# Transposes spread singly among the products of a graph network's node and edge steps

## The chip, the cores and the metric

The kernel runs on one core of one Trainium2 chip. The metric is the device time of one execution in microseconds (us); lower is better. One execution was also taken with the hardware profiler, which gives every instruction's start, duration and what ended the idle time before it.

## The reference, cut to what matters

Three layers of a graph network run over 10,000 nodes of 512 features and 5,000 edges, all in 32-bit floats:

```
def _sage_conv(x, src, dst, Wp, bp, Wl, bl, Wr):
    h = jax.nn.relu(x @ Wp.T + bp)
    agg = jax.ops.segment_sum(h[src], dst, num_segments=N)
    cnt = jax.ops.segment_sum(jnp.ones((src.shape[0],), x.dtype), dst, num_segments=N)
    agg = agg / jnp.maximum(cnt, 1.0)[:, None]
    return agg @ Wl.T + bl + x @ Wr.T
...
h = jnp.maximum(_layernorm(x, axis=-1), 0.0)
# three of these in a row; after layers 0 and 1: relu, layernorm, times g, plus be
x = x + (the last layer's result)
```

## The kernel before, in words

**Tiles.** A layer has 79 node tiles of 128 rows and then 40 edge tiles of 125 rows. A node tile is loaded, normalised on ScalarE (`xn`, L697), stored to `node_x` for the edges to gather from, and turned on TensorE: four transposes of 128x128 (`node_turn`, L492; the transposes at L498), one for each chunk of 128 features, into one bank of PSUM. ScalarE rounds the bank to a high part (`xt_high`, L677) and VectorE takes the remainder (`xt_low`, L791 in layer 0, L794 later). The product with Wr (`node_product`, L502) then takes, for each of the four chunks, three matmuls of 512 columns (L512 low times high, L513 high times low, L514 high times high), which add up in one bank. VectorE adds the bias (`node_out`, L835; in layer 2 the residual, L832) and SyncE's queue stores the rows.

**Edge tiles.** An edge tile is gathered by GpSimd (L419) into `rows_in`, turned in the same way (`edge_turn`, L556; transposes at L564), split into high and low (L707, L910 or L913), and used by `project` (L568) in groups of four tiles: each of the four calls for a group makes one quarter of the output features, 12 matmuls at L579 to L581. `edge_product` (L585, 12 matmuls at L598 to L600) and `edge_sum` (L603) follow, then GpSimd adds the rows into the node table (L431), one tile's transfer after the other.

**Order.** Each engine has its own order, written out by hand, and waits on counting semaphores. A node step `i` puts on TensorE: turn tile i+2, product of tile i, and in layer 0 extra work. On ScalarE it puts std of tile i+6, `xt_high` of tile i+2, and the norm of tile i+5. On VectorE it puts `xt_low` of tile i+2 first, then `node_out` of i-1, statistics of i+8, small operations, and in layer 0 the extra work. SyncE's queue stores tile i-1 once `n_out` allows it, and in layer 2 loads the residual of tile i+3 behind the same wait (L338).

**The extra work that matters here.** In layer 0, steps 46 to 65 look up how many edges each edge's node has. TensorE makes two small matmuls a step behind the product (`lookup`, L529, two calls; matmuls at L535), VectorE reads them in its next step (`read_count`, L879, at L881). Call 2j may not start before the reading of call 2j-2 is done, since it writes the same bank:

```
if t >= 2:
    pe.wait_ge(count_read, t - 1)
```

On VectorE step i reads the two calls of step i-1, as the last entries of the step:

```
if l == 0 and STEP_LOOKUP <= i - 1 < STEP_LOOKUP + EDGE_TILES // LOOKUPS:
    for q in range(LOOKUPS):
        read_count((i - 1 - STEP_LOOKUP) * LOOKUPS + q)
```

Of the kernel before, what the change touches and what calls it, by code (L numbers as in the profile page):

```python
# [5 lines left out]
P = 128  # L6
# [11 lines left out]
IN_RING = 8  # L18
XN_RING = 4
# [6 lines left out]
GROUP = 4  # L26
# [7 lines left out]
AHEAD_TURN = 2  # L34
# [19 lines left out]
def sage_kernel(nc, x_in, src_cols, dst_cols, dst_rows, weights, out):  # L54
# [4 lines left out]
    EDGE_TILES, EDGE_ROWS = dst_rows.shape  # L59
    K = D // P  # L60
    NODE_TILES = -(-N // P)
# [9 lines left out]
    with ExitStack() as ctx:  # L71
        def sb(name, shape, dt):
            return ctx.enter_context(nc.sbuf_tensor(name, shape, dt))

        def sem(name):
            return ctx.enter_context(nc.semaphore(name))

        def sems(name, n):
            return [sem(f"{name}{i}") for i in range(n)]
# [5 lines left out]
        bank = [ctx.enter_context(nc.psum_tensor(f"bank{i}", [P, 512], F32)) for i in range(8)]  # L85
# [14 lines left out]
        ident = sb("ident", [P, P], F32)  # L100
# [35 lines left out]
        rows_in = sb("rows_in", [P, IN_RING, D], F32)  # L136
        xn = sb("xn", [P, XN_RING, D], F32)
# [63 lines left out]
        n_xn = sem("n_xn")  # L201
        n_xn_stored = sems("n_xn_stored", XN_RING)
        n_turned = sem("n_turned")
        n_xt_high = sem("n_xt_high")
        n_xt_low = sem("n_xt_low")
# [6 lines left out]
        e_gathered = sems("e_gathered", IN_RING)  # L212
        e_turned = sem("e_turned")
        e_xt_high = sem("e_xt_high")
        e_xt_low = sem("e_xt_low")
# [12 lines left out]
        def turns(t, ring):  # L228

            return t // ring + 1  # L230

        def uses(count, ring, slot):

            return -(-(count - slot) // ring)
# [5 lines left out]
        def edge_dma(l, t, ring):  # L240
            return DMA * (l * uses(EDGE_TILES, ring, t % ring) + turns(t, ring))
# [9 lines left out]
        def is_node(t):  # L251
            return 0 <= t < NODE_TILES

        def node_xt(buf, t):

            s = t % XT_RING
            return buf[1][:, s * K * P:(s + 1) * K * P]
# [6 lines left out]
        def edge_bank(t):  # L264

            return (t + NODE_TILES) % 2
# [222 lines left out]
        def _(pe):  # L489
            pe.wait_ge(consts, CONSTS)  # L490

            def node_turn(l, t):  # L492
                n = l * NODE_TILES + t
                pe.wait_ge(n_xn, n + 1)
                if n >= 2:
                    pe.wait_ge(n_xt_low, n - 1)
                for k in range(K):
                    last = nc.tensor.transpose(bank[t % 2][:, k * P:(k + 1) * P],  # L498
                                               xn[:, t % XN_RING, k * P:(k + 1) * P], ident[:])
                last.then_inc(n_turned, 1)  # L500

            def node_product(l, t):  # L502
                n = l * NODE_TILES + t
                pe.wait_ge(n_xt_low, n + 1)
                if n >= 4:
                    pe.wait_ge(n_out, n - 3)
                high, low = (node_xt(b, t).rearrange("p (k m) -> p k m", k=K) for b in (xt_high, xt_low))
                for k in range(K):
                    if t == 0:
                        pe.wait_ge(low_done["r"], K * l + k + 1)  # L510
                    psum = bank[4 + t % 4][:]
                    nc.tensor.matmul(psum, low[:, k, :], w_high["r"][:, k, :], start=(k == 0), stop=False)  # L512
                    nc.tensor.matmul(psum, high[:, k, :], w_low["r"][:, k, :], start=False, stop=False)  # L513
                    last = nc.tensor.matmul(psum, high[:, k, :], w_high["r"][:, k, :],  # L514
                                            start=False, stop=(k == K - 1))
                last.then_inc(n_product, 1)

            def count(t):
                pe.wait_ge(hot_done, t + 1)
                nc.tensor.matmul(bank[2][:, 0:P], hot[:, t % HOT_RING, 0, :], hot[:, t % HOT_RING, 1, :],  # L520
                                 start=(t == 0), stop=(t == EDGE_TILES - 1)).then_inc(counted, 1)

            def steps_of_counts():
                pe.wait_ge(steps_made, 1)
                pe.wait_ge(counts_copied, 1)
                nc.tensor.matmul(bank[3][:, 0:P], step_down[:], counts[:], start=True, stop=True
                                 ).then_inc(steps_product, 1)

            def lookup(t):  # L529
                pe.wait_ge(reached_done, t + 1)  # L530
                if t == 0:
                    pe.wait_ge(steps_copied, 1)
                if t >= 2:
                    pe.wait_ge(count_read, t - 1)
                nc.tensor.matmul(bank[2 + t % 2][0:EDGE_ROWS, 0:P], reached[:, t % STEP_RING, :], count_steps[:],  # L535
                                 start=True, stop=True).then_inc(looked_up, 1)
# [10 lines left out]
            def shift_z(l):  # L547
# [5 lines left out]
                                            start=(k == 0), stop=(k == K - 1))  # L553
                last.then_inc(shift_z_product, 1)

            def edge_turn(l, t):  # L556
                e = l * EDGE_TILES + t
                pe.wait_ge(e_gathered[t % IN_RING], edge_dma(l, t, IN_RING))
                if t >= 2:
                    pe.wait_ge(e_xt_low, e - 1)  # L560
                else:
                    pe.wait_ge(n_xt_low, NODE_TILES * (l + 1) - 1 + t)
                for k in range(K):
                    last = nc.tensor.transpose(bank[edge_bank(t)][:, k * P:(k + 1) * P],  # L564
                                               rows_in[:, t % IN_RING, k * P:(k + 1) * P], ident[:])
                last.then_inc(e_turned, 1)

            def project(l, g, m):  # L568
                h = l * EDGE_TILES + g * GROUP + m
                if m == 0:  # L570
                    pe.wait_ge(e_xt_low, l * EDGE_TILES + (g + 1) * GROUP)
                    if g == 0:
                        pe.wait_ge(low_done["p"], K * (l + 1))
                if h >= 2:
                    pe.wait_ge(e_h_pre, h - 1)
                high, low = (b[g % 2][:].rearrange("p (k c) -> p k c", k=K) for b in (xt_high, xt_low))
                psum, cols = bank[2 + m % 2][:, 0:GROUP_ROWS], slice(m * P, (m + 1) * P)
                for k in range(K):
                    nc.tensor.matmul(psum, w_high["p"][:, k, cols], low[:, k, :], start=(k == 0), stop=False)  # L579
                    nc.tensor.matmul(psum, w_high["p"][:, k, cols], high[:, k, :], start=False, stop=False)  # L580
                    last = nc.tensor.matmul(psum, w_low["p"][:, k, cols], high[:, k, :],  # L581
                                            start=False, stop=(k == K - 1))
                last.then_inc(e_projected, 1)
# [29 lines left out]

            for l in range(LAYERS):
                for i in NODE_STEPS:
                    if is_node(i + AHEAD_TURN):
                        node_turn(l, i + AHEAD_TURN)
                    if is_node(i):
                        node_product(l, i)
                    if l == 0 and 0 <= i < EDGE_TILES:  # L620
                        count(i)
                    if l == 0 and i == STEP_PLACES + 1:
                        steps_of_counts()
                    if l == 0 and STEP_LOOKUP <= i < STEP_LOOKUP + EDGE_TILES // LOOKUPS:
                        for q in range(LOOKUPS):
                            lookup((i - STEP_LOOKUP) * LOOKUPS + q)
                    if l and i == STEP_SHIFT_P:
                        shift_p(l)
                    if 0 <= i - (NODE_TILES - EDGE_TURNS_AT) < EDGE_TURNS_AT:
                        edge_turn(l, i - (NODE_TILES - EDGE_TURNS_AT))  # L630

                for t in range(EDGE_TURNS_AT, GROUP):
                    edge_turn(l, t)
                for m in range(GROUP):
                    project(l, 0, m)
                    edge_turn(l, GROUP + m)
                for s in range(EDGE_TILES):
                    g, i = s // GROUP, s % GROUP
                    if s + 2 * GROUP < EDGE_TILES:
                        edge_turn(l, s + 2 * GROUP)  # L640
                    if g + 1 < GROUPS:
                        project(l, g + 1, i)
                    edge_product(l, s)
                    if s >= 1:
                        edge_sum(l, s - 1)
                edge_sum(l, EDGE_TILES - 1)
                if l + 1 < LAYERS:
                    shift_z(l + 1)
# [397 lines left out]
```

## Time and profile before

| | |
|---|---|
| median of 3 runs | 1701.73 us (1700.76 to 1707.29) |
| the profiled execution's own time | 1701.59 us |
| span of its instructions | 1699.7 us |
| mean granted TensorE clock | 0.974 of full speed |
| TensorE matmuls busy | 93% |
| VectorE / ScalarE / GpSimd busy | 54% / 44% / 30% |

The span runs from the first to the last instruction; 1.9 us lie outside of it. A matmul's recorded duration includes its latency, and matmuls overlap, so the distance from one start to the next tells what one costs. Weight loads (PEld) run beside matmuls.

### The profile page before, as it was taken

The numbers are of one execution on the slowest core, as the hardware profiler recorded it, in microseconds if no ns is written. First come the engines' busy times: TensorE is split into PE (matmuls) and PEld (weight loads), VectorE is DVE, ScalarE is ACT, GpSimd is POOL, SyncE is SP. The second block draws the span as 40 slices with busy tenths as digits, with TensorE's granted clock in tenths as the row PEclk, the third lists the DMA queues.
The fourth block names the chain that finished last, engine by engine and source line by source line (L and its number), as shares of the span: only waits on it lengthen the run. The fifth ranks groups of instructions, "written<-read, shape, count | busy, mean of one in ns | idle before, by whom it ended". The sixth has DMA issues, their size and how long they took to land.

```text
span 1699.7 us, 22083 instructions
## 1 busy us (share of the span) xinstructions
PE 1586.3 (93%) x7594; PEld 1285.0 (76%) x7594; DVE 918.5 (54%) x2233; ACT 755.2 (44%) x1386; POOL 502.3 (30%) x468
## 2 busy tenths in 40 slices
PE   6999989899999399999989999949999998999994
PEld 4777778788888278888878888837888887888883
DVE  6777665445444166766544544416666664444441
ACT  4555333233333275766523433327676652333331
POOL 3432221243422200100034433223353444343222
PEclk9999999999999799999999999988999999999997
DMA  9777554444433477777545443349999984444433
GB/s 332 274 244 242 190 182 172 121 90 87 78 53 44 101 265 240 246 245 247 188 140 108 81 87 54 41 77 346 312 337 326 330 278 149 74 81 81 63 43 44
DMA packets 148086, 284.42 MB, mean 167 GB/s; under 512 B 18281, under 2 KB 18281, under 8 KB 147977
## 3 DMA queue, kind: packets, MB, share of 16 engines
q1 hardware_dynamic: 121096, 220.09, 37.9%
q0 software_dynamic: 26880, 62.93, 20.9%
q8 instruction: 62, 1.02, 0.3%
q14 instruction: 48, 0.39, 0.1%
HBM read 126.69 MB, written 156.26 MB: 166 GB/s over the span
## 4 chain that ended last, share of the span: by engine, by line
PE 85%; DMA 7%; DVE 3%; ACT 2%; issue 2%; SPq 0%; POOL 0%; POOLq 0%; ACTq 0%
PE bank L512 12%; PE bank L513 12%; PE bank L514 12%; PE bank L579 6%; PE bank L580 6%; PE bank L581 6%; PE bank L498 6%; PE bank L600 6%; PE bank L598 6%; PE bank L599 6%; DMA node_z<-rows_out,into_i 4%; PE bank L564 3%; PE bank L610 1%; PE bank L611 1%; DMA out<-rows_out,into_i 1%
## 5 line engine op out<-in xcount | busy, mean ns | idle before, releaser
L512 PE MATMUL bank<-w_high_r,xt_low 128*128 128x512 f32 x948 | 396.2, 418 | 0.0
L513 PE MATMUL bank<-w_low_r,xt_high 128*128 128x512 f32 x948 | 375.8, 396 | 0.0
L514 PE MATMUL bank<-w_high_r,xt_high 128*128 128x512 f32 x948 | 375.5, 396 | 0.0
L715 ACT ACTIVATE h_high<-h_pre 128x500 fp32r<-128x500 f32 x120 | 74.6, 622 | 334.0 <-DVE h_pre L921 334.0
L431 POOL DMA_INDIRECT node_z<-rows_out,into_i x80 | 126.0, 1575 | 321.2 <-ACT rows_out L735 260.0
L514 PEld LDWEIGHTS bank<-w_high_r,xt_high 128*128 128x128 f32 x948 | 179.4, 189 | 42.7
L498 PE MATMUL bank<-ident,xn 128*128 128x128 f32 x948 | 146.7, 279 | 67.5 <-ACT xn L697 61.4
L579 PE MATMUL bank<-xt_low,w_high_p 128*128 128x500 f32 x480 | 197.8, 412 | 9.9 <-DVE xt_low L913 6.6
L513 PEld LDWEIGHTS bank<-w_low_r,xt_high 128*128 128x128 f32 x948 | 180.4, 190 | 31.8
L512 PEld LDWEIGHTS bank<-w_high_r,xt_low 128*128 128x128 f32 x948 | 180.0, 190 | 32.0
L794 DVE TENSOR_TENSOR xt_low<-bank,xt_high 128x512 fp32r<-128x512 f32 x158 | 109.3, 692 | 165.4 <-ACT xt_high L677 164.8
L419 POOL DMA_INDIRECT rows_in<-node_x,src_i x120 | 117.7, 981 | 253.3 <-DMA node_x<-xn 167.2
L677 ACT ACTIVATE xt_high<-bank 128x512 fp32r<-128x512 f32 x237 | 141.5, 597 | 113.4 <-PE bank L498 113.4
L697 ACT ACTIVATE xn<-rows_in,off,rstd 128x512 f32<-128x512 f32 x237 | 190.6, 804 | 0.0
L600 PE MATMUL bank<-w_high_l,h_high 128*125 128x512 f32 x480 | 189.6, 395 | 0.0
L598 PE MATMUL bank<-w_high_l,h_low 128*125 128x512 f32 x480 | 189.5, 395 | 0.0
L599 PE MATMUL bank<-w_low_l,h_high 128*125 128x512 f32 x480 | 189.4, 395 | 0.0
L580 PE MATMUL bank<-xt_high,w_high_p 128*128 128x500 f32 x480 | 189.2, 394 | 0.0
L581 PE MATMUL bank<-xt_high,w_low_p 128*128 128x500 f32 x480 | 188.2, 392 | 0.0
L498 PEld LDWEIGHTS bank<-ident,xn 128*128 128x128 f32 x948 | 116.6, 144 | 93.8 <-ACT xn L697 54.2
L803 DVE BATCH_NORM_STATS2 stats<-rows_in 128x6 f32<-128x512 f32 x237 | 161.9, 684 | 47.2 <-ACT rows_in L683 39.3
L932 DVE TENSOR_TENSOR p_low<-bank,p_high 125x512 fp32r<-125x512 f32 x120 | 83.0, 692 | 170.7 <-ACT p_high L722 170.7
(93 smaller groups left out, 2232.5 us busy)
## 6 DMA issues: line engine op xcount, KB each, us to landing
node_x<-xn SPq DMA_DIRECT2D x237, 256.0 KB, 2.7
node_z<-rows_out SPq DMA_DIRECT2D x159, 256.0 KB, 2.0
rows_in<-node_z SPq DMA_DIRECT2D x158, 256.0 KB, 4.1
out<-rows_out SPq DMA_DIRECT2D x80, 256.0 KB, 3.3
rows_in<-x SPq DMA_DIRECT2D x78, 256.0 KB, 2.9
residual<-x SPq DMA_DIRECT2D x78, 256.0 KB, 4.1
stage<-Wr_t SPq DMA_DIRECT2D x12, 256.0 KB, 4.0
stage<-Wp_t SPq DMA_DIRECT2D x3, 1024.0 KB, 7.7
```

The lines of the kernel that those rows point to most:

```text
L498: last = nc.tensor.transpose(bank[t % 2][:, k * P:(k + 1) * P], xn[:, t % XN_RING, k * P:(k + 1) * P], ident[:])
L512: nc.tensor.matmul(psum, low[:, k, :], w_high["r"][:, k, :], start=(k == 0), stop=False)
L513: nc.tensor.matmul(psum, high[:, k, :], w_low["r"][:, k, :], start=False, stop=False)
L514: last = nc.tensor.matmul(psum, high[:, k, :], w_high["r"][:, k, :], start=False, stop=(k == K - 1))
L579: nc.tensor.matmul(psum, w_high["p"][:, k, cols], low[:, k, :], start=(k == 0), stop=False)
L580: nc.tensor.matmul(psum, w_high["p"][:, k, cols], high[:, k, :], start=False, stop=False)
L581: last = nc.tensor.matmul(psum, w_low["p"][:, k, cols], high[:, k, :], start=False, stop=(k == K - 1))
L598: nc.tensor.matmul(psum, low, w_high["l"][:, m, :], start=(m == 0), stop=False)
L599: nc.tensor.matmul(psum, high, w_low["l"][:, m, :], start=False, stop=False)
L600: last = nc.tensor.matmul(psum, high, w_high["l"][:, m, :], start=False, stop=(m == K - 1))
L697: S.activation(xn[:, to, :], rows_in[:, slot, :], ACT.Identity, bias=off[:, slot:slot + 1], scale=rstd[:, slot:slot + 1]).then_inc(n_xn, 1)
L803: V.bn_stats(stats[:, slot, :], rows_in[:, slot, :]).then_inc(n_stats, 1)
```

## The change

In node steps the four transposes of tile i+2 no longer stand in a row ahead of the product of tile i. One of them stands ahead of each chunk's three matmuls. In edge steps the four transposes of a later tile stand in the same way inside `project`. The signal that a tile is turned still comes from its fourth transpose. The waits of the first transpose now stand behind those of the product that it sits in. Numbers and kinds of instructions, buffers and the order of all other engines stay as they are. Tiles that have no product to sit in (tiles 0 and 1 of a layer's nodes, tiles 0 to 3 of its edges) are still turned in a row. That leaves 77 node tiles and 36 edge tiles a layer with single transposes.

```diff
-            def node_turn(l, t):
+            def node_turn(l, t, k):
                 n = l * NODE_TILES + t
-                pe.wait_ge(n_xn, n + 1)
-                if n >= 2:
-                    pe.wait_ge(n_xt_low, n - 1)
-                for k in range(K):
-                    last = nc.tensor.transpose(bank[t % 2][:, k * P:(k + 1) * P],
-                                               xn[:, t % XN_RING, k * P:(k + 1) * P], ident[:])
-                last.then_inc(n_turned, 1)
-
-            def node_product(l, t):
+                if k == 0:
+                    pe.wait_ge(n_xn, n + 1)
+                    if n >= 2:
+                        pe.wait_ge(n_xt_low, n - 1)
+                last = nc.tensor.transpose(bank[t % 2][:, k * P:(k + 1) * P],
+                                           xn[:, t % XN_RING, k * P:(k + 1) * P], ident[:])
+                if k == K - 1:
+                    last.then_inc(n_turned, 1)
+
+            def node_product(l, t, turned):
...
                 for k in range(K):
+                    if is_node(turned):
+                        node_turn(l, turned, k)
...
-            def project(l, g, m):
+            def project(l, g, m, turned):
...
                 for k in range(K):
+                    if turned < EDGE_TILES:
+                        edge_turn_chunk(l, turned, k)
...
                 for i in NODE_STEPS:
-                    if is_node(i + AHEAD_TURN):
-                        node_turn(l, i + AHEAD_TURN)
                     if is_node(i):
-                        node_product(l, i)
+                        node_product(l, i, i + AHEAD_TURN)
+                    elif is_node(i + AHEAD_TURN):
+                        for k in range(K):
+                            node_turn(l, i + AHEAD_TURN, k)
...
                 for m in range(GROUP):
-                    project(l, 0, m)
-                    edge_turn(l, GROUP + m)
+                    project(l, 0, m, GROUP + m)
                 for s in range(EDGE_TILES):
                     g, i = s // GROUP, s % GROUP
-                    if s + 2 * GROUP < EDGE_TILES:
-                        edge_turn(l, s + 2 * GROUP)
                     if g + 1 < GROUPS:
-                        project(l, g + 1, i)
+                        project(l, g + 1, i, s + 2 * GROUP)
```

`edge_turn_chunk(l, t, k)` is one pass of the old loop of `edge_turn`, with the waits at k = 0 and the signal at k = 3.

TensorE in a node step of layer 0 that has lookups (L535), before: the four transposes (L498) follow the lookups at once, and the tile's 12 product matmuls come behind.

```order
L535 MATMUL bank<-count_steps,reached 125x128 [waits count_read,reached_done] x2
L498 MATMUL bank<-ident,xn 128x128 [waits n_xt_low,n_xn]
L498 MATMUL bank<-ident,xn 128x128 x3
L512 MATMUL bank<-w_high_r,xt_low 128x512 [waits n_out,n_xt_low]
L513 MATMUL bank<-w_low_r,xt_high 128x512
L514 MATMUL bank<-w_high_r,xt_high 128x512
```

The same place after the change (the lookup is at L539, transposes at L499, products at L516 to L518), with the first two chunks shown; the third and fourth read like the second, and the next step's lookups follow the fourth.

```order
L539 MATMUL bank<-count_steps,reached 125x128 [waits count_read,reached_done] x2
L499 MATMUL bank<-ident,xn 128x128 [waits n_xn,n_xt_low,n_out]
L516 MATMUL bank<-w_high_r,xt_low 128x512
L517 MATMUL bank<-w_low_r,xt_high 128x512
L518 MATMUL bank<-w_high_r,xt_high 128x512
L499 MATMUL bank<-ident,xn 128x128
L516 MATMUL bank<-w_high_r,xt_low 128x512
```

What moved is the fourth transpose, which carries the signal: it stood ahead of all 12 product matmuls and now stands behind nine of them.

TensorE at the start of a layer's edge steps, before: tile 3 is turned, the first `project` (L579 to L581) runs, and tile 4 is turned behind it.

```order
L564 MATMUL bank<-ident,rows_in 128x128 [waits e_xt_low,e_gathered3]
L564 MATMUL bank<-ident,rows_in 128x128 x3
L579 MATMUL bank<-xt_low,w_high_p 128x500 [waits low_done_p,e_xt_low]
L580 MATMUL bank<-xt_high,w_high_p 128x500
L581 MATMUL bank<-xt_high,w_low_p 128x500
```

The same place after (transposes at L568, `project` at L590 to L592):

```order
L568 MATMUL bank<-ident,rows_in 128x128 [waits e_xt_low,e_gathered3]
L568 MATMUL bank<-ident,rows_in 128x128 x3
L568 MATMUL bank<-ident,rows_in 128x128 [waits e_gathered4,e_xt_low,low_done_p]
L590 MATMUL bank<-xt_low,w_high_p 128x500
L591 MATMUL bank<-xt_high,w_high_p 128x500
L592 MATMUL bank<-xt_high,w_low_p 128x500
```

Each tile's first transpose now waits for what the `project` around it waits for. The same holds where the first group ends and the second begins: tiles 7 and 8 were turned in a row between the two, and are now turned inside the one and inside the other.

## Rows read from the trace of the kernel before

**Rows 1.** The page, busy time: us, share of the span, instructions.
```profile
PE 1586.3 (93%) x7594; PEld 1285.0 (76%) x7594; DVE 918.5 (54%) x2233; ACT 755.2 (44%) x1386; POOL 502.3 (30%) x468
```

**Rows 2.** Timeline, one row of transposes in layer 1: start us, us, engine, line.
```profile
603.14 0.60 PE L498 MATMUL bank<-ident,xn 128*128 128x128 f32 x4
...
603.36 0.14 PEld L498 LDWEIGHTS bank<-ident,xn 128*128 128x128 f32 x1
603.47 0.19 PEld L512 LDWEIGHTS bank<-w_high_r,xt_low 128*128 128x128 f32 x1
603.58 0.19 PEld L513 LDWEIGHTS bank<-w_low_r,xt_high 128*128 128x128 f32 x1
```

**Rows 3.** Timeline, one node step with lookups, layer 0.
```profile
200.82 0.72 PE L535 MATMUL bank<-count_steps,reached 128*125 128x128 f32 x4 [0.43 <-DVE unused L881]
...
201.38 0.60 PE L498 MATMUL bank<-ident,xn 128*128 128x128 f32 x4
...
202.02 0.60 ACT L677 ACTIVATE xt_high<-bank 128x512 fp32r<-128x512 f32 x1 [1.39 <-PE bank L498]
...
202.65 0.69 DVE L791 SCALAR_TENSOR_TENSOR xt_low<-bank,xt_high 128x512 fp32r<-128x512 f32 x1 [1.71 <-ACT xt_high L677]
...
203.21 0.39 PE L512 MATMUL bank<-w_high_r,xt_low 128*128 128x512 f32 x1
...
203.91 0.40 PE L512 MATMUL bank<-w_high_r,xt_low 128*128 128x512 f32 x1
...
204.38 0.40 PE L514 MATMUL bank<-w_high_r,xt_high 128*128 128x512 f32 x1
...
204.98 0.34 DVE L881 SCALAR_TENSOR_TENSOR unused<-column_no,lo_f,bank 125x128 bf16<-125x128 f32 x1
205.21 0.72 PE L535 MATMUL bank<-count_steps,reached 128*125 128x128 f32 x4 [0.43 <-DVE unused L881]
```

**Rows 4.** Waits: engine, line, waited for: us in total, times, longest.
```profile
PE bank L535 <- DVE unused L881: 8.1, 19, 0.4
```

**Rows 5.** Timeline, last node steps of layer 2, into the edges.
```profile
1402.92 0.68 DVE L832 TENSOR_TENSOR rows_out<-bank,residual 128x512 f32<-128x512 f32 x1
...
1404.01 0.43 SPq L338 DMA_DIRECT2D residual<-x  x1
...
1405.95 1.29 POOL L467 TENSOR_TENSOR residual<-residual,bias_z 128x512 f32<-128x512 f32 x1 [0.93 <-DMA residual<-x]
1407.39 1.02 POOL L419 DMA_INDIRECT rows_in<-node_x,src_i  x1
...
1411.36 0.66 PE L564 MATMUL bank<-ident,rows_in 128*128 128x128 f32 x4 [0.89 <-DMA rows_in<-node_x,src_i]
```

**Rows 6.** Timeline, layer 1: first gather, first edge transposes.
```profile
846.51 1.02 POOL L419 DMA_INDIRECT rows_in<-node_x,src_i  x1 [130.78 <-DMA node_x<-xn]
...
856.02 0.60 PE L564 MATMUL bank<-ident,rows_in 128*128 128x128 f32 x4
```

**Rows 7.** Timeline, edge steps of layer 0, from the first group to the second.
```profile
318.01 1.04 PE L564 MATMUL bank<-ident,rows_in 128*128 128x128 f32 x8
...
320.23 1.26 DVE L910 SCALAR_TENSOR_TENSOR xt_low<-bank,xt_high 128x500 fp32r<-128x500 f32 x2
320.95 0.49 PE L579 MATMUL bank<-xt_low,w_high_p 128*128 128x500 f32 x1 [1.91 <-DVE xt_low L910]
```

**Rows 8.** Timeline, TensorE right behind that, and at layer 1's same place.
```profile
322.13 0.62 PE L580 MATMUL bank<-xt_high,w_high_p 128*128 128x500 f32 x1
322.55 0.62 PE L581 MATMUL bank<-xt_high,w_low_p 128*128 128x500 f32 x1
...
878.69 0.49 PE L579 MATMUL bank<-xt_low,w_high_p 128*128 128x500 f32 x1 [1.91 <-DVE xt_low L913]
```

**Rows 9.** Windows: stretch, us, busy by engine, PEclk (granted), DMA share, GB/s.
```profile
321.80:325.20 3.40, 3.40 (x10) 2.71 (x9) 0.00 (x0) 0.00 (x0) 0.00 (x0) 0.50 0.28 78
870.00:890.00 20.00, 18.09 (x88) 14.74 (x87) 10.63 (x18) 6.10 (x11) 4.81 (x5) 1.00 0.24 66
```

More of the change, by code:

```diff
@@ L554, in shift_z, with edge_turn_chunk @@
                 last.then_inc(shift_z_product, 1)
-            def edge_turn(l, t):
[L557 to L562, printed above, removed]
+            def edge_turn_chunk(l, t, k):
+                e = l * EDGE_TILES + t
+                if k == 0:
+                    pe.wait_ge(e_gathered[t % IN_RING], edge_dma(l, t, IN_RING))
+                    if t >= 2:
+                        pe.wait_ge(e_xt_low, e - 1)
+                    else:
+                        pe.wait_ge(n_xt_low, NODE_TILES * (l + 1) - 1 + t)
+                last = nc.tensor.transpose(bank[edge_bank(t)][:, k * P:(k + 1) * P],
+                                           rows_in[:, t % IN_RING, k * P:(k + 1) * P], ident[:])
+                if k == K - 1:
+                    last.then_inc(e_turned, 1)
+            def edge_turn(l, t):
                 for k in range(K):
-                    last = nc.tensor.transpose(bank[edge_bank(t)][:, k * P:(k + 1) * P],
-                                               rows_in[:, t % IN_RING, k * P:(k + 1) * P], ident[:])
-                last.then_inc(e_turned, 1)
-            def project(l, g, m):
+                    edge_turn_chunk(l, t, k)
+            def project(l, g, m, turned):
                 h = l * EDGE_TILES + g * GROUP + m
```

## The prediction

> **What bounds the kernel now.** I read the page's busy times first: TensorE is busy for 93% of the span and no other engine for more than 54% [rows 1]. So the question is what the change does to the distance between TensorE's instructions, and to its few waits. Next I read the timeline of one row of transposes, to see what a transpose costs and what sets that cost. Then the waits, for places where TensorE waits for another engine within the same step. There are few, but one is systematic: 19 times the lookups of layer 0 wait for VectorE's reading of the earlier ones [rows 4]. Last I read the timeline at the borders between node and edge steps, and the granted clock around them.
>
> **The change part by part.**
>
> *What a transpose costs, in a row and alone.* The four transposes begin at 603.14 us. The weight load of the last one is recorded at 603.36, the load for the product behind it at 603.47, and the load for the second product at 603.58 [rows 2]. The loads follow each other at 0.11 us, and a load begins when the matmul before it begins. So the first product begins at about 603.58, and the four cost 603.58 - 603.14 = 0.44 us, 0.11 each. What sets the 0.11 is the next weight load, which can't start before the short transpose has begun. That holds for the fourth too: between its start (603.47) and the product's lies 0.11, the load of the product's own weights. A single transpose among products is exactly this fourth one: its own load hides under the product ahead of it, and the load of the next product lies open behind it. Four singles are then 4 x 0.11 = 0.44 us, as before. I take a change of nothing for the 3 x (77 + 36) = 339 tiles. The rows are good to about 0.005 us a transpose, which is up to 7 us over 1356 of them in either direction; the range takes it in. The Trainium skill ("TensorE: Matmul & The Clock Gate", section on LDWEIGHTS) has a weight load take its columns over 1.2 GHz, 107 ns for 128, and these rows agree. The same page (section "Back-to-back issue gap") gives about 81 ns for each 128-column matmul in a stream of load and matmul pairs; by that figure the sum would lose an estimated 1356 x 0.03 = 40 us. The trace shows 0.11 in the row and at its end, so I go by the trace.
>
> *The signal comes later.* The fourth transpose of tile i+2 used to begin 3 x 0.11 = 0.33 us behind the first. Now three chunks stand between: a transpose, 0.11, and three products, 203.91 - 203.21 = 0.70 [rows 3]. The fourth begins 3 x 0.81 = 2.43 us behind the first, 2.10 later than before. ScalarE's and VectorE's work on that tile moves by 2.10, and so does everything queued behind it on those engines in that step. The product that needs the tile comes two steps later, at least 4.1 us behind the fourth transpose (the rest of its own step, 0.81, and one whole step of 4 x 0.81), and the two conversions take some 1.6 us (0.60 and 0.69 with the hand-overs) [rows 3], so the products themselves don't wait. The same holds in the edge steps, where more work lies between.
>
> *Lookups: this is the large term.* In the steps with lookups TensorE does wait for something that VectorE does behind `xt_low` in the same step. The chain closes on itself. Lookups begin at 200.82 and the first transpose 0.56 later, at 201.38. The fourth begins at 201.71. ScalarE starts at 202.02, VectorE at 202.65, VectorE reads the earlier lookups as the last of its step (204.98), and the next lookups begin at 205.21, which is 3.50 behind the fourth transpose [rows 3]. The period is 0.56 + 0.33 + 3.50 = 4.39 us, as the two lookups show (205.21 - 200.82). After the change the middle term is 2.43 in place of 0.33, and nothing else in the chain moves, because each engine's order is the same: 0.56 + 2.43 + 3.50 = 6.49 us. The products hide less of it now. What is queued behind the waiting lookups is the whole next step of TensorE. The waits are 19 [rows 4], so this costs 19 x 2.10 = 39.9 us.
>
> *The clock in those steps.* TensorE's idle time in each of them grows. The last product begins 0.11 + 2 x 0.235 = 0.58 behind the fourth transpose and is recorded for 0.40, so the idle time is 3.50 - 0.98 = 2.5 us in place of 0.43 [rows 3]. The granted clock of layer 0's edge steps fell to 0.50 (1.2 of 2.4 GHz) for 3.4 us right after TensorE had stood for 1.9 us [rows 7, 9]. There the products stood 0.42 us apart [rows 8] in place of 0.23, so a fall costs 3.4 x (1 - 0.23 / 0.42) = 1.5 us. At the same place in layer 1, after the same wait of 1.91, it didn't fall [rows 8, 9]. So the bounds are no fall in 19 steps and a fall in each, 0 and 29 us. I take 5 falls, 7.5 us. The wait is longer than the one that had a fall once and none once, but only part of each step, and each fall is followed by some 4 us of dense work. A chosen number, not a worked one.
>
> *Layer 2, into the edges.* VectorE's `node_out` of tile 74 (1402.92) stands behind `xt_low` of tile 77 in its step. It releases the load of the last residual (1404.01), which GpSimd adds (1405.95) before its first gather (1407.39), and the first edge transposes wait for that gather (1411.36) [rows 5]. Each link is released by the one before, so all of it moves by 2.10 us: plus 2.1. In layers 0 and 1 the first gather starts 9.5 us ahead of its use (846.51 and 856.02) [rows 6], where 4.0 are needed (1407.39 to 1411.36) [rows 5]. A delay of 2.1 is hidden there.
>
> *From the first edge group to the second.* TensorE turned tiles 7 and 8 at 318.01 while it had to wait anyway for tile 7's `xt_low`, which itself stands behind work that follows the last `project` of the first group (320.23, then TensorE at 320.95) [rows 7]. The eight transposes, 0.87 us, cost nothing there. After the change both tiles are turned inside the projects, on the path: plus 0.88 a layer, 2.6 us in all. The wait behind grows from 1.91 to 2.8, and the one of layer 2 before its first gather from 0.89 to 3.0, so I add one fall of the clock, 1.5 us.
>
> *Sum.* 39.9 + 7.5 + 2.1 + 2.6 + 1.5 = 53.6 us. The profiled execution's own time is 1701.6 (span and 1.9 us around it), 0.1 below the median of the three, so I forecast 1701.6 + 53.6 = 1755 us, 3.2% slower.
>
> **The rivals.**
>
> *The single transpose hides its cost (faster).* If TensorE could load two sets of weights ahead, the product's load would hide too, and a transpose among products would cost only its own pass, 0.23 x 128/512 = 0.06 us. That is 0.05 less for each of 1356, minus 68 us, and with the 53.6 above 1687. It decides above 0.04 us saved on each. The Trainium skill's same page says that the queue can pull weight loads ahead of matmuls in flight, which by itself would leave room for this. Against it: in the rows each load starts only once the matmul before it has started [rows 2], also where the engine had nothing else to do. Chance 0.05.
>
> *The lookups don't wait longer (no change).* Then the change would cost 2.1 + 2.6 + 1.5, 1708. It takes that the readings don't depend on the turned tile. The order on VectorE has them behind `xt_low`, and the idle time before the lookups is ended by them 19 times [rows 4]. Chance 0.04.
>
> *The clock falls in most of the lookup steps.* 15 falls in place of 5 add 15 us: 1770. A longer wait in every step speaks for it; the fall that stayed out in layer 1 speaks against it. Chance 0.10.
>
> *The clock does not fall at all.* 1755 - 9 = 1746. It lies inside the forecast. The forecast with its sizes between 1743 and 1765 has a chance of 0.78. The rest, 0.03, is for things not seen.
>
> **How the numbers follow.** The low end takes no fall and a few of the before's falls gone, with a transpose slightly cheaper: 1742. The high end takes the transpose at 0.003 more and some 10 falls: 1768. Half a per cent, 8.5 us, is about what a measurement of this kernel can tell from no change. Faster 0.05 (the first rival), same 0.05 (the second and a part of the unseen), slower 0.90.
>
> **What the profile after would show.** The lookups 6.5 us apart in place of 4.39 (8 or more where the clock fell), with 2.5 us of idle time before them, ended by VectorE's reading. VectorE's share in that stretch falls, its order doesn't change. A single transpose followed by its product's load at 0.11. TensorE's first edge transposes of layer 2 wait about 3 us for the gather, those of layers 0 and 1 not at all. The wait at the second edge group about 2.8 us. The prediction is wrong if the spacing from one chunk to the next is not 0.81, or if the lookups stay near 4.4 us apart.

## The result, and the profile after

The changed kernel takes 1756.15 us (median of 4 runs, 1755.6 to 1761.13) against 1702.08 us before: a ratio of 1.0318, with a 95% interval of 1.029 to 1.0347. It is 54 us slower. The profiled execution took 1756.45 us with a span of 1754.6.

The page's busy times answer to [rows 1]. TensorE does the same 7594 matmuls, and its share falls from 93% to 91%: the added time is mostly waiting.

```profile
PE 1597.2 (91%) x7594; PEld 1247.4 (71%) x7594; DVE 911.7 (52%) x2233; ACT 765.9 (44%) x1386; POOL 498.6 (28%) x468
```

The timeline of weight loads in a node step of layer 1 answers to [rows 2]; the columns are start, duration, engine, line.

```profile
720.30 0.14 PEld L499 LDWEIGHTS bank<-ident,xn 128*128 128x128 f32 x1
720.53 0.19 PEld L516 LDWEIGHTS bank<-w_high_r,xt_low 128*128 128x128 f32 x1
720.64 0.19 PEld L517 LDWEIGHTS bank<-w_low_r,xt_high 128*128 128x128 f32 x1
```

A single transpose's load (720.30) lies under the product ahead of it. The transpose starts at 720.53, where the product's load is recorded. The next load is recorded 0.11 later (720.64), and I take that as the product's real start, since the other loads in this stretch begin with the matmul ahead of them; the product's own record begins at 720.56 already. The sum bears this out: one chunk of transpose and three products takes 0.81 us, and three products take 0.70. So a single transpose costs 0.11 us, as one in a row does.

A node step with lookups, timeline of TensorE, ScalarE and VectorE, answers to [rows 3]:

```profile
209.70 0.72 PE L539 MATMUL bank<-count_steps,reached 128*125 128x128 f32 x4 [2.51 <-DVE unused L890]
...
210.26 0.27 PE L499 MATMUL bank<-ident,xn 128*128 128x128 f32 x1
...
212.69 0.27 PE L499 MATMUL bank<-ident,xn 128*128 128x128 f32 x1
...
212.99 0.60 ACT L686 ACTIVATE xt_high<-bank 128x512 fp32r<-128x512 f32 x1 [3.49 <-PE bank L499]
...
213.62 0.69 DVE L800 SCALAR_TENSOR_TENSOR xt_low<-bank,xt_high 128x512 fp32r<-128x512 f32 x1 [3.80 <-ACT xt_high L686]
...
215.95 0.34 DVE L890 SCALAR_TENSOR_TENSOR unused<-column_no,lo_f,bank 125x128 bf16<-125x128 f32 x1
...
216.18 0.61 PE L539 MATMUL bank<-count_steps,reached 128*125 128x128 f32 x3 [2.53 <-DVE unused L890]
```

From the lookups to the first transpose 0.56, from the first to the fourth 212.69 - 210.26 = 2.43, from the fourth to the next lookups 3.49: the period is 6.48 us. The middle term was 0.33 before; the other two are unchanged to 0.01. The list of waits has the same 19 waits as [rows 4], with 47.9 us in place of 8.1:

```profile
PE bank L539 <- DVE unused L890: 47.9, 19, 2.5
```

The windows of the stretch with the lookups, and of one of the five falls of the clock in it (the column behind POOL is the granted clock):

```profile
178.00:302.00 124.00, 78.61 (x361) 59.23 (x360) 48.21 (x180) 28.78 (x56) 20.06 (x34) 0.93 0.35 117
...
201.50:204.90 3.40, 3.10 (x10) 2.66 (x11) 0.43 (x4) 0.11 (x1) 1.18 (x2) 0.50 0.65 219
```

The falls begin at 181.0, 201.5, 228.8, 256.1 and 283.4 us, each 3.4 us long, so about every fourth step has one. The windows around each of the five show a granted clock of 0.50 or 0.51.

Layer 2 on its way into the edges (VectorE's output of tile 74, the last residual, the gather, the first edge transposes), timeline, answers to [rows 5]:

```profile
1456.54 0.68 DVE L841 TENSOR_TENSOR rows_out<-bank,residual 128x512 f32<-128x512 f32 x1
...
1457.63 0.43 SPq L338 DMA_DIRECT2D residual<-x  x1
...
1459.73 1.30 POOL L467 TENSOR_TENSOR residual<-residual,bias_z 128x512 f32<-128x512 f32 x1 [1.25 <-DMA residual<-x]
...
1461.18 1.02 POOL L419 DMA_INDIRECT rows_in<-node_x,src_i  x1
...
1464.79 1.12 PE L568 MATMUL bank<-ident,rows_in 128*128 128x128 f32 x4 [2.83 <-DMA rows_in<-node_x,src_i]
```

The wait for the first gather is 2.83 us in place of 0.89. And the second edge group of layer 0, TensorE's timeline, answers to [rows 7]: the wait for tile 7's `xt_low` is 2.78 in place of 1.91, and tile 8's first transpose stands behind it.

```profile
366.31 0.33 PE L568 MATMUL bank<-ident,rows_in 128*128 128x128 f32 x1 [2.78 <-DVE xt_low L919]
```

Where the time went can be read from the start of the same instruction in both timelines. The mark for the nodes is the third product matmul of a tile's first chunk, the mark for the edges the second matmul of the first `edge_sum`:

| instruction | before, us | after, us | later by |
|---|---|---|---|
| layer 0, product of tile 47 | 175.98 | 175.42 | -0.6 |
| layer 0, product of tile 66 | 259.30 | 305.88 | 46.6 |
| layer 0, first edge sum | 334.31 | 378.49 | 44.2 |
| layer 1, product of tile 78 | 856.92 | 901.62 | 44.7 |
| layer 1, first edge sum | 890.47 | 938.99 | 48.5 |
| layer 2, product of tile 77 | 1407.97 | 1459.46 | 51.5 |
| layer 2, first edge sum | 1447.30 | 1501.49 | 54.2 |

47.1 of the 54.9 us of span are added within 19 steps of layer 0 (46.6 + 0.6, rounded).

Away from all waits and falls the step itself changed a little. The same marks 50 steps apart, from tile 20 to tile 70:

| | before, us | after, us |
|---|---|---|
| layer 1 | 670.40 to 831.56, 161.2 | 713.82 to 875.82, 162.0 |
| layer 2 | 1224.67 to 1385.84, 161.2 | 1277.16 to 1437.16, 160.0 |

That is 0.017 us a step more in one layer and 0.023 less in the other, about 0.005 us a transpose either way. Why the two layers differ is not known.

### The profile page after: what moved, and what is told of

It reads as the page before. It is cut to its first block, busy times and chain, and to the rows that moved or that the text cites. A ratio compares the mean times of both kernels' runs of the same rounds, so it can differ in the third digit from the quotient of the medians.

```text
span 1754.6 us, 22082 instructions
## 1 busy us (share of the span) xinstructions
PE 1597.2 (91%) x7594; PEld 1247.4 (71%) x7594; DVE 911.7 (52%) x2233; ACT 765.9 (44%) x1386; POOL 498.6 (28%) x468
## 4 chain that ended last, share of the span: by engine, by line
PE 86%; DMA 6%; DVE 3%; ACT 2%; issue 2%; SPq 0%; POOL 0%; POOLq 0%; ACTq 0%
PE bank L516 12%; PE bank L518 12%; PE bank L517 12%; PE bank L590 6%; PE bank L592 6%; PE bank L591 6%; PE bank L499 6%; PE bank L611 6%; PE bank L609 6%; PE bank L610 6%; DMA node_z<-rows_out,into_i 4%; PE bank L568 3%; DMA out<-rows_out,into_i 1%; PE bank L621 1%; PE bank L622 1%
## 5 line engine op out<-in xcount | busy, mean ns | idle before, releaser
L516 PE MATMUL bank<-w_high_r,xt_low 128*128 128x512 f32 x948 | 459.1, 484 | 0.0
L518 PE MATMUL bank<-w_high_r,xt_high 128*128 128x512 f32 x948 | 379.2, 400 | 0.0
L499 PE MATMUL bank<-ident,xn 128*128 128x128 f32 x948 | 261.6, 280 | 66.3 <-ACT xn L706 60.3
L516 PEld LDWEIGHTS bank<-w_high_r,xt_low 128*128 128x128 f32 x948 | 183.8, 194 | 81.3 <-issue 3.6
L590 PE MATMUL bank<-xt_low,w_high_p 128*128 128x500 f32 x480 | 224.4, 467 | 0.0
L499 PEld LDWEIGHTS bank<-ident,xn 128*128 128x128 f32 x948 | 136.1, 144 | 108.2 <-ACT xn L706 50.8
L518 PEld LDWEIGHTS bank<-w_high_r,xt_high 128*128 128x128 f32 x948 | 180.7, 191 | 43.1
L592 PE MATMUL bank<-xt_high,w_low_p 128*128 128x500 f32 x480 | 187.8, 391 | 0.0
L517 PEld LDWEIGHTS bank<-w_low_r,xt_high 128*128 128x128 f32 x948 | 185.5, 196 | 1.0
L697 ACT ACTIVATE std<-mean,eps 128x1 f32<-128x1 f32 x237 | 69.7, 294 | 215.1 <-DVE mean L817 215.0
```

## The experiments

The kernel before took 1698.13 us, in one run, on the chip on which the kernel with only the edge steps and the three with half passes ran, and 1702.88 us (median of 16 runs) on the chip of all the others. Only the first, third, fourth and fifth kernel below ran more than once. The 16 runs of the kernel before span 1698.8 to 1708.6, so a few us between single runs say nothing.

**Only the node steps.** The edge half of the change is undone:

```diff
-                    project(l, 0, m, GROUP + m)
+                    project(l, 0, m, EDGE_TILES)
+                    edge_turn(l, GROUP + m)
...
+                    if s + 2 * GROUP < EDGE_TILES:
+                        edge_turn(l, s + 2 * GROUP)
                     if g + 1 < GROUPS:
-                        project(l, g + 1, i, s + 2 * GROUP)
+                        project(l, g + 1, i, EDGE_TILES)
```

> Single transposes in the node steps alone; the edge steps are as before. Theory (the closed chain of layer 0's lookups grows by 2.10 us a step, and the clock falls in about 5 of those steps): 1702 + 39.9 + 7.5 + 2.1 (first gather of layer 2) = about 1751 us, with the lookups 6.49 us apart. Rival (the loss is spread over all tiles, so that nodes and edges share it by their 231 and 108 tiles): 1702 + 54 x 231/339 = 1739 us, and the lookups near 4.4 us apart.

Measured: 1758.19 us, ratio 1.0306 (1.0269 to 1.0342). The list of waits has the lookups' as in the full change:

```profile
PE bank L539 <- DVE unused L893: 47.9, 19, 2.5
```

The node half alone makes the whole slowdown within the interval; the spread over tiles (1739) is out. The four runs lie between 1750 and 1760. The profiled one, at 1760.17, is 9 us above the 1751 expected, and it has six falls in the lookups' stretch, where five were expected, and eight elsewhere outside the layers' ends, where the kernel before has four. Five falls more are 7.5 us of the 9.

**Only the edge steps.** The node half is undone: the four transposes stand ahead of the product (`alone` is False throughout).

```diff
                 for i in NODE_STEPS:
+                    alone = False
+                    if is_node(i + AHEAD_TURN) and not (alone and is_node(i)):
+                        for k in range(K):
+                            node_turn(l, i + AHEAD_TURN, k)
                     if is_node(i):
-                        node_product(l, i, i + AHEAD_TURN)
-                    elif is_node(i + AHEAD_TURN):
-                        for k in range(K):
-                            node_turn(l, i + AHEAD_TURN, k)
+                        node_product(l, i, i + AHEAD_TURN if alone else -1)
```

> Single transposes in the edge steps alone; the node steps are as before. Theory: only the cover at the second edge group is lost, 3 x 0.88 = 2.6 us, and up to two falls of the clock more or less: 1705 us, between 1702 and 1708, lookups 4.39 us apart. Rival (the loss is spread over all tiles): 1702 + 54 x 108/339 = 1719 us.

Measured: 1704.64 us in one run, with a span 3.0 us longer than before. The waits of the lookups are back:

```profile
PE bank L539 <- DVE unused L891: 8.2, 19, 0.4
```

The one run of the kernel before on that chip took 1698.13, so the time alone doesn't tell 3 us from 6. This execution has five falls, one more than the kernel before. 1719 is out in either reading.

**Rows again in the steps with lookups.** The full change, but 20 of the 231 node tiles with single transposes go back to a row:

```diff
+                    alone = not (l == 0 and STEP_LOOKUP <= i < STEP_LOOKUP + EDGE_TILES // LOOKUPS)
```

(the lines below it as in the experiment above).

> The changed kernel, but in steps 46 to 65 of layer 0, those with lookups, the four transposes stand in a row ahead of the product again. Theory: the lookups come back to 4.39 us apart with 0.43 us of idle time, no fall of the clock there, and 47 us return: 1756 - 47 = about 1709 us. Rival (the single transposes themselves are slow): only 20 of 339 tiles are put back, so 3 us return, 1753 us.

Measured: 1712.4 us, ratio 1.0063 (1.0044 to 1.0081). TensorE's timeline has the lookups 4.38 us apart (201.62 and 206.00), with the old idle time ahead of them:

```profile
201.62 0.72 PE L539 MATMUL bank<-count_steps,reached 128*125 128x128 f32 x4 [0.43 <-DVE unused L891]
...
206.00 0.72 PE L539 MATMUL bank<-count_steps,reached 128*125 128x128 f32 x4 [0.43 <-DVE unused L891]
```

20 tiles bring back 44 of 54 us. Forecast were 47; this execution has eight falls outside the layers' ends, where the full change has six outside the lookups. The other 319 tiles with single transposes stand in a kernel that is 0.6% slower than before.

**The reading first.** The full change, and VectorE reads the lookups of the step before at the front of its step:

```diff
+                    if l == 0 and STEP_LOOKUP <= i - 1 < STEP_LOOKUP + EDGE_TILES // LOOKUPS:
+                        for q in range(LOOKUPS):
+                            read_count((i - 1 - STEP_LOOKUP) * LOOKUPS + q)
                     if is_node(i + AHEAD_TURN):
                         node_xt_low(l, i + AHEAD_TURN)
...
-                    if l == 0 and STEP_LOOKUP <= i - 1 < STEP_LOOKUP + EDGE_TILES // LOOKUPS:
-                        for q in range(LOOKUPS):
-                            read_count((i - 1 - STEP_LOOKUP) * LOOKUPS + q)
```

> The changed kernel, with VectorE's reading of the lookups moved from the end of its step to the front, ahead of xt_low. Theory: the reading no longer waits for the turned tile, the chain is open, and a step with lookups lasts what TensorE's own work lasts, 3.25 us and 0.48 for the lookups, 3.73 in place of 6.49. 19 x 2.76 = 52 us return and the 7.5 of the falls: about 1696 us, faster than both kernels. Rival (what holds the lookups is the turned tile's conversion on ScalarE or the bank, not the place of the reading on VectorE): the lookups stay 6.49 us apart and the time at 1756 us.

Measured: 1698.86 us, ratio 0.9974 to the kernel before (0.9959 to 0.9988), 57 us less than the change alone. TensorE's timeline, lookups 3.68 us apart and no idle time ahead of them:

```profile
200.28 0.60 PE L539 MATMUL bank<-count_steps,reached 128*125 128x128 f32 x4
...
203.96 0.60 PE L539 MATMUL bank<-count_steps,reached 128*125 128x128 f32 x4
```

The signal of the turned tile is as late here as in the change, and the lookups don't care. It was the place of the reading on VectorE, behind the turned tile's `xt_low`, that turned the late signal into a wait. This shows the mechanism, not only its place. Not all of the 57 us are the change's, though: the same move also takes away the 0.43 us of waiting that the kernel before had in each of these steps, as the next experiment shows.

**The reading first, transposes in a row.** The kernel before with the same move of `read_count`.

> The kernel before, with the same move of the reading alone. Theory: the period of 4.39 us becomes 3.73, 19 x 0.66 = 12.5 us: 1702 - 12.5 = about 1689.5 us, some 6 us faster than the changed kernel with the same move, since the edge groups and the first gather of layer 2 keep their cover. Rival: no change at 1702 us, if the reading isn't what the lookups wait for.

Measured: 1686.95 us, ratio 0.9916 (0.9883 to 0.9948): the fastest version, ahead of both kernels. TensorE's timeline, 3.67 us apart:

```profile
199.61 0.60 PE L535 MATMUL bank<-count_steps,reached 128*125 128x128 f32 x4
...
203.28 0.60 PE L535 MATMUL bank<-count_steps,reached 128*125 128x128 f32 x4
```

19 x (4.39 - 3.67) = 13.7 us of the 15.9 are the lookups; the rest is within a fall or two of the clock (this execution has three, the kernel before four). With the readings out of the way the single transposes still lose 12 us to the row (1698.86 against 1686.95). Of these the lost cover at the edge groups and the late gather of layer 2 are some 4; the profiled executions have six falls of the clock against three, some 5 more. Most of the rest is in the plain steps: 50 of them take 162.0 us in layers 1 and 2 with single transposes and 161.2 in a row, which comes to some 2.5 us over the two layers. This stands in the two profiled executions; why the step is longer is not known.

**Tiles 7 and 8 in a row.** On the kernel with single transposes and the readings first:

```diff
-                    project(l, 0, m, GROUP + m)
+                    project(l, 0, m, GROUP + m if m + 1 < GROUP else EDGE_TILES)
                 for s in range(EDGE_TILES):
+                    if s == 0:
+                        edge_turn(l, 2 * GROUP - 1)
+                        edge_turn(l, 2 * GROUP)
                     if g + 1 < GROUPS:
-                        project(l, g + 1, i, s + 2 * GROUP)
+                        project(l, g + 1, i, s + 2 * GROUP if s else EDGE_TILES)
```

> The changed kernel with the readings first (1699 us), in which tiles 7 and 8 of each layer's edges are turned in a row again, between the first group's last project and the second group's first. Theory (these eight transposes lost the wait that covered them): from the last product of the nodes to the first edge product 0.88 us less in each layer, apart from the clock, and the wait behind the transposes back at 1.91 us in place of 2.8 and more. Rival (the wait sets the end and only moves): no difference between the two positions.

Measured: 1696.00 us in one run. TensorE's timeline in layer 0 has the wait back at 1.91:

```profile
302.87 1.03 PE L568 MATMUL bank<-ident,rows_in 128*128 128x128 f32 x8
305.81 0.50 PE L590 MATMUL bank<-xt_low,w_high_p 128*128 128x500 f32 x1 [1.91 <-DVE xt_low L922]
```

The distance from tile 78's product to the first edge sum in layer 1 separates this term from the clock's. The two are sorted by the falls within it:

| kernel | tiles 7, 8 | falls of the clock | us |
|---|---|---|---|
| before | in a row | 0 | 33.55 |
| only the node steps | in a row | 2 | 36.67 |
| this one | in a row | 2 | 36.42 |
| rows again with lookups | single | 1 | 35.86 |
| the reading first | single | 1 | 35.82 |
| the full change | single | 2 | 37.37 |
| only the edge steps | single | 2 | 37.44 |

Two falls cost 3.0 us (36.5 - 33.55), and the lost cover 0.8 (37.4 - 36.55). Layer 0 has the cover by itself: the same distance without any fall is 34.26 in the full change (344.23 to 378.49) and 33.54 in a row (296.86 to 330.40, in the half-load kernel below, whose layer 0 is that of the kernel before).

**The last nine node steps of layer 2 in a row.** On the kernel with the readings first:

```diff
+                    alone = not (l == LAYERS - 1 and i >= NODE_TILES - 9)
```

> The changed kernel with the readings first, in which the last nine node steps of layer 2 turn their tiles in a row again. Theory (the late residual holds the first gather): TensorE's wait for that gather falls from 3.0 to 0.9 us and about 2 us return there. Rival (the gather is late because of the transfers' load): the wait stays near 3 us.

Measured: 1700.07 us in one run. The wait for the first gather, TensorE's timeline:

```profile
1407.56 0.66 PE L568 MATMUL bank<-ident,rows_in 128*128 128x128 f32 x4 [0.81 <-DMA rows_in<-node_x,src_i]
```

0.81 in place of 2.7: the late residual held the gather. The total doesn't show it: it is one run, and its execution had ten falls of the clock where the one with the readings first had six.

**What sets the 0.11 us of a transpose.** Five kernels with smaller transposes in layers 1 and 2; each leaves out half of the nodes or features there, so they serve for timing alone. First half the load, in the kernel before (in a row) and in the one with the readings first (single):

```diff
+                    rows = P // 2 if l else P
-                    last = nc.tensor.transpose(bank[t % 2][:, k * P:(k + 1) * P],
-                                               xn[:, t % XN_RING, k * P:(k + 1) * P], ident[:])
+                    last = nc.tensor.transpose(bank[t % 2][0:rows, k * P:(k + 1) * P],
+                                               xn[:, t % XN_RING, k * P:k * P + rows], ident[:])
```

> The kernel before (transposes in a row), in which in layers 1 and 2 each node transpose takes in only 64 of its chunk's 128 features: its weight load has 64 columns, its pass still 128; the other 64 are left out, so the output of these layers is not the reference's. Theory (a transpose in a row lasts as long as the next weight load): the first three of a row fall from 0.11 to about 0.06 us, the fourth stays at 0.11, since the product's load has 128 columns: 154 tiles x 0.15 = 23 us less, 1679 us. Rival (the pass sets the 0.11): no change, 1702 us.

> The changed kernel with the readings first, with the same half loads in layers 1 and 2 (64 of each chunk's 128 features turned, the rest left out). Theory: nothing changes against 1699 us, because a single transpose's load lies under the product ahead of it and its 0.11 is the product's load behind it. Rival (the transpose's own load or pass is what costs): up to 154 x 4 x 0.05 = 31 us less, 1668 us.

Measured: 1702.08 us in a row, 1693.78 us single. The loads in a row, timeline of weight loads:

```profile
704.59 0.33 PEld L499 LDWEIGHTS bank<-ident,xn 128*64 128x64 f32 x3
704.91 0.19 PEld L513 LDWEIGHTS bank<-w_high_r,xt_low 128*128 128x128 f32 x1
```

Three of the transposes' loads and the product's load still start 0.11 apart (704.59 to 704.91), though the transposes' now have 64 columns. My theory expected 0.06 and 23 us less: it fell. The single one stays as expected at 0.11 from transpose to product; its 5 us less are those of one run, which had one fall less than the execution that it stands beside, and are not explained further.

Then half the pass (64 nodes), in a row, with all 128 columns of load and with 64, and single with all 128. The nodes lie on the partitions, so half the pass also means 64 partitions in place of 128:

```diff
+                    cols = P // 2 if l else P
+                    last = nc.tensor.transpose(bank[t % 2][:, k * P:k * P + cols],
+                                               xn[0:cols, t % XN_RING, k * P:(k + 1) * P], ident[0:cols, 0:cols])
```

> The kernel before (transposes in a row), in which in layers 1 and 2 each node transpose passes only 64 of the tile's 128 nodes: its pass has 64 columns, its weight load still 128; the other nodes are left out, so the output is not the reference's. With half loads the row kept its 0.11 us. Theory A (the pass of 128 columns sets the 0.11, the load hides): the first three of a row fall to about 0.06 us where the load allows it. Theory B (load and pass each take 0.11 by themselves): nothing changes here, 1702 us.

> The same with both halved: 64 nodes and 64 features of each transpose in layers 1 and 2, the rest left out. Theory B (load and pass each take 0.11 by themselves, for 128 columns): only here does the spacing in the row fall, to about 0.06 us for the first three, 154 x 0.15 = 23 us less, 1679 us. Theory C (a transpose has a fixed cost of 0.11 whatever its size): no change, 1702 us.

> The changed kernel with the readings first, with half passes in layers 1 and 2 (64 of the tile's 128 nodes turned, the rest left out). Theories B and A with the product's own load behind each transpose: the distance from a transpose to its product stays at 0.11 us and the time near 1699 us. If the pass alone set it, the distance would fall to about 0.06, 31 us less.

Measured: 1726.59, 1719.87 and 1893.26 us, all three slower than any of the theories said. The timeline of weight loads of the first, in a row with 128 columns of load:

```profile
704.16 0.19 PEld L515 LDWEIGHTS bank<-w_high_r,xt_high 128*128 128x128 f32 x1
704.72 0.33 PEld L499 LDWEIGHTS bank<-ident,xn 64*128 64x128 f32 x4 [0.37 <-issue]
705.11 0.19 PEld L513 LDWEIGHTS bank<-w_high_r,xt_low 128*128 128x128 f32 x1
```

The four loads span 0.33 less one load's 0.14, so they start (0.33 - 0.14) / 3 = 0.06 apart, with 128 columns each. A load of 128 columns does not hold a row at 0.11, and halving the load's columns did not help it. What holds it belongs to the transpose's own pass, as theory A says. Theories B and C, by which the row would have kept its 0.11 here, are out. The passes of 64 columns also use 64 partitions; the runs halve both at once, so which of the two shortens the pass is not separated. And the last product starts at 704.39 and the first such transpose's load only at 704.72, 0.33 later, where the loads in [rows 2] begin as soon as the matmul ahead of them has begun. The single ones show it at each chunk, on TensorE's timeline:

```profile
704.46 0.40 PE L519 MATMUL bank<-w_high_r,xt_high 128*128 128x512 f32 x1
704.79 0.28 PE L500 MATMUL bank<-ident,xn 64*128 64x64 f32 x1
704.99 0.50 PE L517 MATMUL bank<-w_high_r,xt_low 128*128 128x512 f32 x1
...
705.88 0.27 PE L500 MATMUL bank<-ident,xn 64*128 64x64 f32 x1
```

One chunk takes 705.88 - 704.79 = 1.09 us in place of 0.81. Over 154 x 4 chunks that is 172 us, most of the 194 us between this kernel (1893.26) and the one with full transposes (1698.86).

## Why the prediction was right, and where it wasn't

**The period of the lookups.** Forecast 6.49 us, measured 6.48; 19 waits, as forecast. Putting 20 tiles back returned 44 us, and moving the reading returned 57: the mechanism is shown from both sides.

**The clock in those steps.** I took 5 falls, 7.5 us, by choice. There were 5. The stretch from tile 47 to tile 66 grew by 47.1 us against 39.9 + 7.5 = 47.4. The same stretch in the kernel with only the node steps changed had 6 falls and grew by 48.4. So the size was right, and partly by luck: nothing in the prediction gave 5 rather than 0 or 10.

**The first gather of layer 2.** Forecast 2.1 us more wait, measured 2.83 - 0.89 = 1.9; with the last steps in a row again the wait is 0.81.

**The second edge group.** Forecast 0.88 a layer, measured about 0.8. The wait of 2.78 us is the 2.8 forecast.

**Falls elsewhere.** I took one more than before. Outside the lookups and the layers' ends the full change's execution has six (two of them back to back) and before has four, so it was two more. Layer 0's edges lost both of theirs and layer 1's gained two: the table of starts shows it as 46.6 and then 44.2 in layer 0, and as 44.7 and then 48.5 in layer 1. The forecast of one more fall was again a choice. No rule for when a fall comes was tested; the same wait of 1.91 us was followed by one in some executions and not in others.

**The cost of a single transpose.** Forecast 0.11, measured 0.11, with the 0.005 either way that the range allowed for. The reason I gave was wrong; the number did not need it, since it was read from the rows. The step that failed reads "What sets the 0.11 is the next weight load, which can't start before the short transpose has begun." For a row, loads of 64 columns left the 0.11 as it was, and passes of 64 columns on 64 partitions took it to 0.06 under loads of 128 columns. The pass of a 128x128 transpose takes the 0.11 itself. That the prediction saw the time of a load in the rows' 0.11 was a coincidence. The first rival's 0.06 us for a pass had no ground either: if the pass takes 0.11 in front of a product as well, loading two sets of weights ahead would have gained nothing. For that last transpose before a product the two explanations give the same number, and no run here separates them.

**The rivals.** Faster by hidden loads: out. No longer wait for the lookups: out. A fall in most steps: out, 5 in 19.

## What to carry to other kernels

Spreading work to make an engine's stream even also moves the signal at its end. Before doing it, look at what the consumers have queued behind the signalled work, and whether anything there goes back to the producer in the same step: a loop of that kind pays the delay in full at every step (2.1 us, 19 times), while the consumers outside of it hid it here, but for one gather (1.9 us, once). Breaking the loop, here by moving one read to the front of VectorE's step, took 57 us off the changed kernel and 16 off the kernel before; with the loop broken the two orders of the transposes are 12 us apart. And short work that runs inside another wait is free where it stands; moved onto the path, the 0.87 us of eight transposes cost 0.8.

## What the runs showed of the hardware

A transpose whose operands use 64 partitions, behind a product that uses 128, did not get its weights loaded ahead. Its load began 0.33 us after the start of the product ahead of it, where a 128-partition one begins within 0.01 us of it, and the product behind it was held too: 1.09 us for a chunk in place of 0.81. Half the size cost 194 us in the whole kernel. Fewer columns on 128 partitions (the half load) kept the overlap. In a row only the first of four such transposes was held: the other three, 64 partitions behind 64, followed 0.06 apart. So it is the change from 128 to 64 and back that goes with the lost overlap, not the 64. A smaller change keeps the overlap: the sums at the edges use 125 partitions behind products that use 128, and in the kernel before their load begins with the product ahead of them:

```profile
889.99 0.40 PE L600 MATMUL bank<-w_high_l,h_high 128*125 128x512 f32 x1
...
890.00 0.19 PEld L610 LDWEIGHTS bank<-p_low,same 125*125 125x125 f32 x1
```

The Trainium skill ("TensorE: Matmul & The Clock Gate", Part 3) says that a weight load overlaps matmuls in flight only where it uses other rows of the array than they do. Another sentence there lets a load go ahead into a background weight buffer as well, without a condition on rows. The traces here go with that second sentence and against the first: loads on the same 128 rows began within 0.01 us of the matmul ahead in the steps shown, and the load that had to wait was the one on 64 rows behind a product on 128.
